# Causal attention on one core: GpSimd adds the exponentials of two unmasked step pairs per unit, and the expert weights are narrowed in place

## What is computed

```python
# attention, x: (2, 1024, 512), 16 heads of 32
qkv = x @ qkv_w.T + qkv_b                      # q, k with position factors
scores = einsum('bhqd,bhkd->bhqk', q, k) / sqrt(32)
scores = where(causal, scores, -inf)
attn = softmax(scores, axis=-1)
out = einsum('bhqk,bhkd->bqhd', attn, v) @ out_w.T + out_b
...
# experts: weights are used in bfloat16
wg, wu, wd = w_gate.astype(bf16), w_up.astype(bf16), w_down.astype(bf16)
```

## Time and profile before

| | us |
|---|---|
| median of 3 runs | 1585.95 (1582.8 to 1587.18) |
| the profiled execution | 1583.84 |
| its span in the profile | 1582.1 |
| the attention steps within it | 924.3 to 1267.5 |

### The profile page before, as it was taken

The page is one execution under the profiler, slowest core; times in us unless marked ns, Lnnn a source line. Parts: engine busy times, 40 slices in busy tenths (PEclk is TensorE's granted clock), DMA queues, the critical chain, the costliest instruction groups (busy, mean ns, idle before and its releaser), DMA issues. The chain is left out here.

```text
span 1582.1 us, 22556 instructions
## 1 busy us (share of the span) xinstructions
PE 1486.2 (94%) x7696; PEld 1081.7 (68%) x7696; DVE 985.9 (62%) x1906; ACT 614.7 (39%) x1085; POOL 475.2 (30%) x389
## 2 busy tenths in 40 slices
PE   7999879999999999999998999999999898897996
PEld 6788668788888888888886764444444386674554
DVE  6878967855545554552422757777777484466664
ACT  5233444613412431441211134555455635331554
POOL 1233244303421430440432212222222264003770
PEclk9999989999999999999999989999999999999999
DMA  6022346504311430424358683666672666621336
GB/s 213 28 79 84 133 156 222 174 14 138 101 53 53 146 93 0 133 80 161 124 180 235 190 214 94 177 177 177 190 204 86 235 237 246 262 71 58 104 98 226
DMA packets 105277, 223.40 MB, mean 141 GB/s; under 512 B 9376, under 2 KB 35360, under 8 KB 104288
## 3 DMA queue, kind: packets, MB, share of 16 engines
q1 hardware_dynamic: 101440, 211.96, 41.6%
q0 software_dynamic: 3744, 10.23, 2.1%
HBM read 157.54 MB, written 64.36 MB: 140 GB/s over the span
## 5 line engine op out<-in xcount | busy, mean ns | idle before, releaser
L1938 ACT ACTIVATE at_pt<-at_st 128x512 f32<-128x512 f32 (+3 forms) x384 | 164.2, 497 | 140.9 <-PE at_st L1970 139.8
L941 POOL TENSOR_TENSOR ff_w_lo<-ff_raw,ff_w_hi 128x1024 fp32r<-128x1024 f32 x64 | 153.7, 2402 | 208.5 <-ACT ff_w_hi L971 208.5
L115 PE MATMUL op_bank<-ff_x_hi,ff_w_lo 128*128 128x512 f32 x512 | 200.7, 392 | 2.9 <-POOL ff_w_lo L941 2.9
L117 PE MATMUL op_bank<-ff_x_hi,ff_w_hi 128*128 128x512 f32 x512 | 200.3, 391 | 0.0
L116 PE MATMUL op_bank<-ff_x_lo,ff_w_hi 128*128 128x512 f32 x512 | 200.2, 391 | 0.0
L1204 DVE TENSOR_TENSOR ff_h_lo<-ff_hf,ff_h_hi 128x512 f32 (+1 forms) x64 | 149.7, 2339 | 53.4 <-ACT ff_h_hi L1094 53.1
L1970 PE MATMUL at_st<-mx_qp,mx_kp 98*128 98x512 f32 (+3 forms) x288 | 103.5, 391 | 14.3 <-ACT at_pt L1938 10.8
L971 ACT ACTIVATE ff_w_hi<-ff_raw 128x1024 fp32r<-128x1024 f32 x64 | 67.8, 1061 | 118.1 <-PE op_bank L117 118.1
L115 PEld LDWEIGHTS op_bank<-ff_x_hi,ff_w_lo 128*128 128x128 f32 x512 | 96.9, 189 | 23.6 <-issue 3.3
L116 PEld LDWEIGHTS op_bank<-ff_x_lo,ff_w_hi 128*128 128x128 f32 x512 | 96.9, 189 | 20.5
L117 PEld LDWEIGHTS op_bank<-ff_x_hi,ff_w_hi 128*128 128x128 f32 x512 | 96.7, 189 | 20.3
(11 more groups left out here) (452 smaller groups left out, 3359.0 us busy)
## 6 DMA issues: line engine op xcount, KB each, us to landing
ff_raw<-in_Wug SPq DMA_DIRECT2D x64, 512.0 KB, 3.6
at_raw<-in_expert_gu SPq DMA_DIRECT2D x16, 704.0 KB, 12.3
mx_qp<-q_hi SPq DMA_DIRECT2D x12, 512.0 KB, 6.3
mx_kp<-k_hi SPq DMA_DIRECT2D x12, 512.0 KB, 11.9
at_raw<-in_expert_d SPq DMA_DIRECT2D x8, 768.0 KB, 14.1
expert_gu_bf<-at_cast SPq DMA_DIRECT2D x16, 352.0 KB, 11.0
ex_e_gu<-expert_gu_bf SPq DMA_DIRECT2D x8, 704.0 KB, 8.4
tm_ln_res<-in_x SPq DMA_DIRECT2D x4, 1024.0 KB, 5.3
```

The costliest lines, as they stand in the source:

```text
L115: pe.matmul(out, cut_l(ll), cut_r(rh), start=first, stop=False, **kw)
L117: return pe.matmul(out, cut_l(lh), cut_r(rh), start=False, stop=last, **kw)
L941: pool.tensor_tensor(w[j][1][:, :, :, :], raw[:, j], f32(w[j][0][:, :, :, :]), ALU.subtract)\
L1938: act.activation(pt[:, s % PT, h, off:TB], st[(s * HG + h) % ST][:, off:TB], ACT.Exp, scale=SCALE).then_inc(exp_done, 1)
```

## The change

- Of the den group, steps 4 to 7 are left out. In its place POOL adds the exponentials of steps 4 and 5, and of 6 and 7, into one buffer `pair_sum` (a tensor_tensor add of 128 x 2048 floats each), and PE multiplies the ones with each sum: `total_pair`, 0 at the end of step 7 and 1 at the end of step 10. A unit has so 10 den groups where it had 12. (The constants call the steps by `TT`, which is 4.)
- `pt` holds four steps (`PT` = LAG + 2). ACT's exponentials of steps 8 and 9 wait for the first sum, those of 10 and 11 for the second; the second sum waits until the products of the first are done.
- The bfloat16 weights are cast into the same bytes as their raw floats. A load of a narrow piece therefore waits for the store of the piece three before, where it waited for the cast. SP's list of a unit is now: the three narrow loads, the q, k and v parts, the three narrow stores, the attended block, the maxima, the other attended block.
- ACT waits at its first copy for the stores of v, on which SP waits already.

```diff
-    PT = LAG + 1
+    PT = LAG + 2
+    PAIR_STEPS = [(TT, TT + 1), (TT + 2, TT + 3)]
+    SUM_AT = {step: n for n, (_, step) in enumerate(PAIR_STEPS)}
+    TOTAL_AT = {TT + 3: 0, TT + 6: 1}
+    SUMS = len(PAIR_STEPS)
...
@@ sync
             for u in range(UNITS):
+                for n in range(PER_UNIT):
+                    narrow.load(sp, u * PER_UNIT + n)
                 if u + 2 < UNITS:
                     at_least(sp, pv_done, u * NS)
                     mx.load(sp, u + 2)
...
                 for n in range(PER_UNIT):
-                    if u:
-                        narrow.store(sp, (u - 1) * PER_UNIT + n)
-                    narrow.load(sp, u * PER_UNIT + n)
+                    narrow.store(sp, u * PER_UNIT + n)
                 if u:
                     store(u - 1, 1)
...
@@ gpsimd
                     if s == TT:
                         for n in range(PER_UNIT):
                             narrow.narrow(pool, u * PER_UNIT + n)
+                    if s in SUM_AT:
+                        n = u * SUMS + SUM_AT[s]
+                        first, second = PAIR_STEPS[SUM_AT[s]]
+                        pool.wait_ge(exp_done, (u * NS + second + 1) * HG)
+                        at_least(pool, totalled, n)
+                        pool.tensor_tensor(pair_sum[:, :, :], pt[:, first % PT, :, :], pt[:, second % PT, :, :], ALU.add)\
+                            .then_inc(summed, 1)
+                        pool.wait_ge(summed, n + 1)
...
@@ scalar
-                at_least(act, pv_done, u * NS + s - LAG)
+                at_least(act, pv_done, u * NS + s - PT + 1)
+                if s >= 2 * TT:
+                    act.wait_ge(summed, u * SUMS + (s - 2 * TT) // 2 + 1)
...
@@ tensor
                 for total, lhs in ((num, None), (den, ones)):
+                    if lhs is not None and TT <= s < 2 * TT:
+                        continue
...
+            def total_pair(u, n):
+
+                pe.wait_ge(summed, u * SUMS + n + 1)
+                for h in range(HG):
+                    mm = pe.matmul(den[h * HD:(h + 1) * HD, :], ones[:, :], pair_sum[:, h, :], start=n == 0, stop=False, skip_group_check=True)
+                mm.then_inc(totalled, 1)
...
                 if g >= LAG:
                     pv(*place(g - LAG))
+                if s in TOTAL_AT:
+                    total_pair(u, TOTAL_AT[s])
...
@@ NarrowWeights
+            self.raw.append(b.sb(f"raw{s}", [P, NM * C]))
+        self.cast = [b.overlay(f"cast{s}", [P, NM * C], homes[s], BF16) for s in range(self.BUFFERS)]
...
-        sp.wait_ge(self.narrowed, n - self.BUFFERS + 1) if n >= self.BUFFERS else None
+        at_least(sp, self.stored[n % self.BUFFERS], n // self.BUFFERS * DMA)
```

More of the change, by code:

```diff
@@ L1811, in attend @@
         pt = b.sb("pt", [P, PT, HG, TB])
-        last_at = b.next_at() - 2 * TT * C * 4
+        last_at = b.next_at() - 2 * TT * C * 4 - HG * TB * 4
         num_sb, den_sb = b.sb("num_sb", [P, QC, TB]), b.sb("den_sb", [P, QC, TB])
@@ L1825, in attend @@
         PER_UNIT = len(narrow.pieces) // UNITS
+        pair_sum = b.sb("pair_sum", [P, HG, TB])
+        summed, totalled = b.sem("summed"), b.sem("totalled")
         out = Outcome(b, src, dst, o_out, o_stored, ow, mx, st[0], last_at, ((UNITS - 2) * NS, (UNITS - 1) * NS))
@@ L1887, in _ @@
                     out.ln.load(sp, 1)
-                    for n in range(PER_UNIT):
-                        narrow.store(sp, u * PER_UNIT + n)
                 store(u, 0)
@@ L1926, in copy_out @@
             def copy_out(u, qc):
+                if u == 0 and qc == 0:
+                    for stored in mx.v_stored:
+                        act.wait_ge(stored, NB * TT // 2 * DMA)
                 act.wait_ge(pv_done, u * NS + ENDS[qc] + 1)
@@ L2084, in __init__ @@
         self.a = a
-        self.raw = [b.sb(f"raw{s}", [P, NM * C]) for s in range(self.BUFFERS)]
-        self.cast = [b.sb(f"cast{s}", [P, NM * C], BF16) for s in range(self.BUFFERS)]
+        homes = []
+        self.raw = []
+        for s in range(self.BUFFERS):
+            homes.append(b.next_at())
+            self.raw.append(b.sb(f"raw{s}", [P, NM * C]))
+        self.cast = [b.overlay(f"cast{s}", [P, NM * C], homes[s], BF16) for s in range(self.BUFFERS)]
         self.loaded = [b.sem(f"loaded{s}") for s in range(self.BUFFERS)]
@@ L2103, in narrow @@
         pool.wait_ge(self.loaded[s], (n // self.BUFFERS + 1) * DMA)
-        at_least(pool, self.stored[s], (n // self.BUFFERS) * DMA)
         pool.tensor_copy(self.cast[s][:, 0:self.cols(n)], self.raw[s][:, 0:self.cols(n)]).then_inc(self.narrowed, 1)
```

## The result

| kernel | median us | runs | ratio to before, 95% interval |
|---|---|---|---|
| before | 1586.57 | 1582.80 to 1587.19 | |
| after | 1610.51 | 1609.86 to 1612.07 | 1.0159 (1.0144 to 1.0174) |

The change makes the kernel slower by 24 us. The direction was as predicted; the time lies above 1598 and outside the range of 1588 to 1607. The profiled execution took 1609.86 us (span 1608.1), 26 more than that of before. In one kernel of the experiments, the one whose gap is filled with two groups, one run of seven took 2897 us, and the ratio goes by the six others.

A forecast was written before the change was run, and what follows sets the result against it. PE, busy 94% of the span, was taken to set the pace. Unit changes of +3.9 us, stalls included, plus +9.6 for clock falls gave +13.5 on 1583.84, 1597.3; the median was forecast at 1598, range 1588 to 1607.

The forecast's parts named there:

- the change without the collision: Multiply never meets the sum: seven units gain 2.2 us and unit 7 gains 0.2, together -15.6 us.
- the stall: Step 6, units 1 to 6: POOL's first sum holds DVE's multiply 3.2 us, delaying PE's fourth piece; +19.5 us together.
- the clock: After PE's 3.4 us gap at step 6 the clock falls in six units, 1.6 us each: +9.6 us.
- over a fall that makes about 0.8 for each of two groups' worth of work, 1.6 us: Steps 6 and 7: half clock over a fall, taken from 4 us falls, costs PE 1.6 us.
- six of 2.0 us (half of 4), 12: Upper bound of the clock's cost: a fall in each of six units, 12 us; the lower bound was 0.
- the undisturbed unit: A unit without collision gains 2.2 us: 1.94 from fewer PE products and 0.3 from DVE's wait at step 11.
- the join: DVE's join of the maxima ends with POOL's second sum, before PE's transpose; costs 0 to 0.3 us, taken as 0.
- It meets, but the clock stays up: Rival: multiply held at step 6, but no clock fall in all or most units; 1588 to 1592 us, chance 0.17.
- The multiply doesn't meet the sum: Rival: weights land so late that DVE's multiply goes before POOL's first sum; 1568 to 1571 us, chance 0.12.
- The rival above my range: Second-order waits: join, step 8 mask and step 10 exponentials late behind the second sum; 1607 to 1614 us, chance 0.07.

The follow-up runs named there:

- the one whose gap is filled with two groups: Changed kernel, plus two unneeded den groups on PE ahead of its fourth piece of step 6 in units 1 to 6; 1616.63 us, 1.0049 of before.
- the waiting sum: Changed kernel, but POOL's first sum of a unit also waits for DVE's multiply of the unit before (units 1 to 7); 1571.58 us, 0.9923 of before.
- the gap filled with three groups: Changed kernel, plus three unneeded den groups on PE ahead of its fourth piece of step 6 in units 1 to 6; 1592.98 us, 1.0059 of before.
- the kernel with one group: Changed kernel, plus one unneeded den group on PE ahead of its fourth piece of step 6 in units 1 to 6; 1607.33 us, 1.0127 of before.
- the group behind the gap: Changed kernel, but units 1 to 6 also make step 4's den group right behind PE's gap and discard it; 1626.67 us, 1.0126 of before.
- the second run of the waiting sum: Changed kernel with POOL's first sum waiting for the previous unit's multiply, repeated on another chip; 1594.64 us, 0.9922 of before.
- the kernel with four adds: Changed kernel, but POOL makes each sum as four adds of 128 x 512, one for each head; 1573.47 us, 0.9917 of before.

## Why the prediction failed, step by step

In us on 1586; measured as steps between the ratios of before, the waiting sum, the gap filled with three groups, and after (1.0000, 0.9923, 1.0059, 1.0159), each good to about 3 us:

| term | predicted | measured |
|---|---|---|
| the change without the collision | -15.6 | -12.2 |
| the stall | +19.5 | +21.6 |
| the clock | +9.6 | +15.9 |
| together | +13.5 | +25.2 |

The filled kernel has the falls of 4 us of its own in units 1 and 4, 1.7 us each, so the table counts some 3 us of the clock's cost as stall: by that the stall is nearer 18 us and the clock 19.

**Right: where and why.** The casts are done by 1080.87, behind the mask of step 3. The sum takes 4.53 us (4.6 forecast). The multiply meets it in all six units, ends 0.55 us behind it, and PE's piece waits 3.3 us, all as worked out from the earlier trace rows. A unit with collision and no fall would be 1.0 us longer than before; it is 43.7 - 42.35 = 1.35.

**Wrong: the length of a fall.** The step that failed is "over a fall that makes about 0.8 for each of two groups' worth of work, 1.6 us". The price of a fall of 4 us was right: 1.5 to 1.7 us by the periods. But I took 4 us from the earlier trace rows, and five of six falls last 10.5 to 11 us and cost 4.2. The bounds, "six of 2.0 us (half of 4), 12", rested on the same length: they end at 1602, and no term of mine led from there to 1607. The trace of before would have warned me. Of the nine falls that I counted in it I showed two of 4 us, but four of the nine last 7 us or more: 7 from 218.5, 14 from 925, 7.5 from 1331 and from 1430. The two gaps nearest to the 3.4 us that I forecast are among them, one of 3.3 us ahead of 1332.5 and one of 3.1 that opens this very stage, with the 14 us behind it:

```profile
921.20:924.20 3.00, 0.00 (x0) 0.00 (x0) 0.68 (x1) 0.13 (x1) 0.13 (x1) 1.00 0.31 87
...
925.00:939.00 14.00, 13.91 (x48) 8.65 (x47) 8.89 (x29) 6.54 (x16) 4.68 (x4) 0.51 0.95 230
```

And ahead of the stretch in which I counted, between 178.5 and 190 us:

```profile
178.50:181.00 2.50, 0.00 (x0) 0.00 (x0) 2.47 (x2) 0.63 (x1) 1.76 (x2) 1.00 0.01 3
181.00:188.00 7.00, 3.66 (x9) 2.94 (x10) 6.73 (x10) 4.08 (x6) 0.25 (x1) 0.51 0.33 113
188.00:190.00 2.00, 2.00 (x11) 1.62 (x10) 1.16 (x3) 0.48 (x1) 0.00 (x0) 1.00 0.34 130
```

A gap of 2.5 us and 7 us near half clock. An upper end from that row, six times half of 7, is 21 us: 1583.84 + 3.9 + 21 is 1608.7 on the profiled execution, 1610.8 with the 2.1 up to the median, and the range would just have held the time. Because the two rows that I showed agreed, I took a spread for a constant.

**Too good: the undisturbed unit.** -1.4 us (42.35 to 40.95) where I had -2.2. I priced a den group at 0.97 us from its start to the next scores; on the path it is worth 0.86, by the starts of the num groups that PE makes in steps 6 and 7 in the timelines of unit 3: 1078.58 and 1082.28 before, 1074.83 and 1077.67 in the kernel where the sum waits, 3.70 against 2.84. The product at step 7 waits 0.17 us for the sum there. And the 0.3 us that PE waited for DVE at step 11 didn't come back: in the kernel where the sum waits it still waits 0.25 us where it had waited 0.35.

**Right by its price: the join.** It takes 1.65 us for 0.18, since it ends with the second sum, and PE's weight load for the transpose waits for it (5.0 us in six units); but the transpose at 1103.31 stands right behind the num group of 1102.32. I had given it 0 to 0.3 and taken 0.

**The rivals.** "It meets, but the clock stays up" is what the kernels with the filled gap do, 1.0059 and 1.0049 of before, or 1595 and 1594 on 1586, where I gave 1588 to 1592. "The multiply doesn't meet the sum" is the kernel in which the sum waits, 1571.58 where 1568 to 1571 were forecast, so just above. The rival above my range named second-order waits, at 0.07; the time came there by another way, a longer fall, that I had shut out with my bounds.

## What to carry to other kernels

Before work goes to GpSimd, list what VectorE does meanwhile with both inputs in SBUF, and give one of the two a wait or a place of its own; here one wait moved the kernel from 1.6% slower to 0.8% faster. A long GpSimd instruction cut into shorter ones lets VectorE in between. A gap on PE has two prices, the stall and the clock behind it, and the second can be the larger: 4.2 us a unit against 2.75 here. So ask of a wait on PE whether it can be kept short or filled, and take the length of a fall as a range from all falls of the trace: the same program had one of 11 us and one of 4 at the same place.

## What the runs showed of the hardware

- Gaps of 2.3 and 3.3 us at the same place, step 6, brought the same fall of 10.5 to 11 us in units 2 to 6, and one of 4 in unit 1; gaps of 0.6 and 1.5 us there by none. (At the turn to the next unit's maxima falls of 4 us stand in some units behind a wait of 0.6 us, in before too.) From the gap's end on, at half clock, PE was busy without a break (9.65 of 9.65 us in the kernel with one group).
- Falls in the attention of these traces last 3.5 to 4, 7 to 7.5 or 10.5 to 11 us; in three runs (before, the group behind the gap, the second run of the waiting sum) one of 14 stands in unit 0. With one den group more behind the gap they lasted 4 to 7.5.
- The same program with the same gap of 2.73 us had a fall of 11 us in one execution and of 4 in another, on another chip, beginning 1.3 us ahead of the gap's end and at it. At step 6 the short falls began in the last 0.4 us of the gap or behind it, the long ones nearly all earlier. What sets that place, and so which length it is going to be, I can't tell from a trace of before; that stays open.
- A POOL copy of 128 x 2048 with one input takes 1.90 us, an add with two 4.5 to 4.6. Both hold a DVE multiply with two SBUF inputs, which then ends 0.54 to 0.55 us behind them. Four adds of a quarter take 5.36 us for 4.6.
- The holding goes both ways: in the kernel with four adds POOL's second add took 1.76 us for 1.28 beside the multiply, and the sum 5.84 for 5.36.
